# Self attentions: the four transfers of the row sums go from SyncE's queue to GpSimd's, one in each unit

## The reference

```python
x = x + attention_with_position_bias(layernorm(x))   # self attention A
x = x + cross_block(layernorm(x), ctx_1024, mask)    # cross attention, self attention S, feed-forward
x = x + experts(layernorm(x))                        # 8 experts, top 2
# in each self attention, for batch b and head h:
probs = softmax(q_h @ k_h.T * SCALING [+ bias_h])    # 256 x 256
out_h = probs @ v_h                                  # 256 x 8
```

## Time and profile before

| | |
|---|---|
| median of three runs | 1294.16 us (1292.65 to 1294.98) |
| the profiled execution's own time | 1292.28 us |
| its span, first to last instruction | 1290.3 us |
| busy: PE, DVE, ACT, POOL | 1077.4, 995.1, 860.7, 406.4 us |
| mean granted TensorE clock | 0.92 of full speed |

### The profile page before, as it was taken

How to read it: one execution, slowest core, us unless ns; L and a number is a source line. 1 busy time by engine, 2 the same in 40 slices (tenths; PEclk the granted TensorE clock), 3 DMA queues, 4 the chain that set the end, 5 groups by cost and what they waited for, 6 DMA issues and landing times. The chain is left out here.

```text
span 1290.3 us, 32652 instructions
## 1 busy us (share of the span) xinstructions
PE 1077.4 (83%) x11660; PEld 576.5 (45%) x11660; DVE 995.1 (77%) x2779; ACT 860.7 (67%) x1764; POOL 406.4 (31%) x832
## 2 busy tenths in 40 slices
PE   5779995699999999999999999997667878539993
PEld 2334443244444444444444444443433445428883
DVE  7458766588889888898888988992777968766664
ACT  3468883087888878877788787785357965425553
POOL 3211213214150230502305023011442515755662
PEclk8689998689999999999999999998878999759997
DMA  6934015523223132231322303100373012301113
GB/s 164 219 70 96 24 29 139 139 65 78 61 55 98 55 79 62 62 95 51 79 62 60 95 27 79 53 5 3 103 148 63 14 46 94 106 13 40 46 48 115
DMA packets 82974, 94.84 MB, mean 73 GB/s; under 512 B 12775, under 2 KB 69039, under 8 KB 82816
## 3 DMA queue, kind: packets, MB, share of 16 engines
q1 hardware_dynamic: 78720, 86.46, 26.7%
q0 software_dynamic: 2496, 5.12, 1.5%
q10 hardware_dynamic: 1600, 1.18, 0.4%
HBM read 66.47 MB, written 27.48 MB: 73 GB/s over the span
## 5 line engine op out<-in xcount | busy, mean ns | idle before, releaser
L1558 DVE TENSOR_REDUCE MG<-bank 128x1 f32<-128x401 f32 (+1 forms) x1024 | 515.4, 566 | 75.2 <-PE bank L1342 73.3
L1478 ACT ACTIVATE PT<-bank 128x512 f32<-128x512 f32 (+1 forms) x624 | 334.7, 597 | 64.2 <-PE bank L1360 63.6
L1360 PE MATMUL bank<-QP,KP 54*128 54x256 bf16 (+1 forms) x1664 | 252.5, 274 | 16.2 <-DVE CAT L1573 4.1
L1342 PE MATMUL bank<-KP,QP 54*128 54x401 bf16 (+1 forms) x1024 | 237.1, 344 | 14.7 <-DMA KP<-ctx_k_parts 9.5
L1380 PE MATMUL bank<-PT,VP 128*9 128x256 f32 (+1 forms) x2688 | 198.2, 368 | 0.8 <-ACT XT L1478 0.8
L1633 POOL TENSOR_TENSOR MP<-MN,ZERO 128x4 bf16<-128x4 f32 x128 | 26.4, 206 | 440.9 <-DVE MN L1565 435.9
L1360 PEld LDWEIGHTS bank<-QP,KP 54*128 54x128 bf16 (+1 forms) x1664 | 110.6, 96 | 108.1 <-ACT PT L1478 24.4
L1342 PEld LDWEIGHTS bank<-KP,QP 54*128 54x128 bf16 x1024 | 75.5, 94 | 125.0 <-DVE MG L1558 93.2
L1004 PE MATMUL bank<-QP,KP 51*128 51x256 bf16 x512 | 97.9, 285 | 39.1 <-DMA QP<-q_parts 12.5
L1478 ACT ACTIVATE XT<-bank 128x512 f32<-128x512 f32 (+1 forms) x208 | 116.2, 599 | 20.3 <-PE bank L1360 19.9
L971 PE MATMUL bank<-KP,QP 51*128 51x256 bf16 x512 | 100.7, 294 | 3.9 <-DVE MG L1099 1.0
(11 more groups left out here) (283 smaller groups left out, 1870.7 us busy)
## 6 DMA issues: line engine op xcount, KB each, us to landing
KP<-ctx_k_parts SPq DMA_DIRECT2D x128, 100.1 KB
ctx_k_parts<-KPARTS SPq DMA_DIRECT2D x16, 600.4 KB, 5.3
KP<-ctx_k_parts SPq DMA_DIRECT2D x128, 59.4 KB
CN<-in_ctx SPq DMA_DIRECT2D x8, 768.0 KB
RAW<-in_w_gate_up SPq DMA_DIRECT2D x8, 512.0 KB, 3.7
QP<-q_parts SPq DMA_DIRECT2D x20, 192.0 KB
ctx_k_parts<-KPARTS SPq DMA_DIRECT2D x16, 200.1 KB, 5.4
UQ<-bias_table SPq DMA_DIRECT2D x4, 768.0 KB, 8.3
```

The source lines that it names most:

```text
L1342: nc.tensor.matmul(GRAIN[n % NG][:, 0:w], k.QP[half, p, b * S + 128 * qt:b * S + 128 * (qt + 1)], k.KP[half, p, a:a + w], start=True, stop ...
L1360: return nc.tensor.matmul(bank[0:rows[t], S * at:S * (at + 1)], k.KP[half, p, 128 * t:128 * t + rows[t]], k.QP[half, p, b * S:(b + 1) * S] ...
L1478: nc.scalar.activation(PT[n % NP][0:rows[t], :], bank_of("s", g, t)[0:rows[t], :], ACT.Exp).then_inc(exp_done, 1)
L1558: nc.vector.tensor_reduce(MG[:, g % 4, 2 * s + qt, chunk:chunk + 1], GRAIN[n % NG][:, 0:w], AX.X, ALU.max).then_inc(m_read, 1)
```

## The change

The four functions issue on GpSimd (`nc.gpsimd.dma_start`, and the waits on GpSimd's stream) instead of SyncE. GpSimd's plan gets an entry behind the split: in step s, for s from 4 to 31, the stage s mod 4 (take, spread, give, place) of batch s // 4 - 1. So there is one transfer in a unit, behind that unit's split. SyncE's loads of the chunks 1 to 3 stand one behind another, in A the mask transfers follow as one run, and in S nothing comes after the loads.

```diff
-        take, spread, give, place = sums
-
-        def place_mask(b):
+        for c in range(1, 4):
+            sp.wait_ge(self.stored[c], 64)
+            load_keys(k, sp, 0, c, qk_in[c])
+            load_queries(k, sp, 0, c, qk_in[c])
+        sp.wait_ge(self.mask_stored, 32)
+        for b in range(B):
             for s in range(2):
                 src = bass.AP(tensor=flat.tensor, offset=b * NCTX, ap=[[B * NCTX, 3], [0, PAIRS], [1, NCTX]])
                 sp.dma_start(k.dC.ap()[b, s, 4 * HD:, :, :], src).then_inc(self.mask_placed, 16)
-
-        sp.wait_ge(self.stored[1], 64)
-        load_keys(k, sp, 0, 1, qk_in[1])
-        take(sp, 0)
-        load_queries(k, sp, 0, 1, qk_in[1])
-        spread(sp, 0)
-        sp.wait_ge(self.stored[2], 64)
-        load_keys(k, sp, 0, 2, qk_in[2])
-        give(sp, 0)
-        load_queries(k, sp, 0, 2, qk_in[2])
-        place(sp, 0)
-        take(sp, 1)
-        sp.wait_ge(self.stored[3], 64)
-        load_keys(k, sp, 0, 3, qk_in[3])
-        spread(sp, 1)
-        load_queries(k, sp, 0, 3, qk_in[3])
-        give(sp, 1)
-        sp.wait_ge(self.mask_stored, 32)
-        place_mask(0)
-        place(sp, 1)
-        for b in range(2, LAST_BATCH):
-            take(sp, b)
-            spread(sp, b)
-            place_mask(b - 1)
-            give(sp, b)
-            place(sp, b)
-        place_mask(LAST_BATCH - 1)
-        place_mask(LAST_BATCH)
         sp.wait_ge(self.mask_placed, 16 * 2 * B)
...
-            if c == 3:
-                take(sp, 0)
-                spread(sp, 0)
             sp.wait_ge(self.stored[c], 64)
             load_keys(k, sp, 2, c, qk_in[c])
-            if c == 3:
-                give(sp, 0)
             load_queries(k, sp, 2, c, qk_in[c])
-        place(sp, 0)
-        for b in range(1, LAST_BATCH):
-            take(sp, b)
-            spread(sp, b)
-            give(sp, b)
-            place(sp, b)
...
-    pool_plan = [("split", 0, 3)]
+    pool_plan = [("split", 0, 3), ("move", 0, 0)]
...
+                elif what == "move":
+                    if PER_BATCH <= step < UNITS and what in actions:
+                        actions[what](step // PER_BATCH - 1, step % PER_BATCH)
...
+        def take_sums(pl, b):
+
+            pl.wait_ge(o_read, PER_BATCH * (b + 1))
             if b > 0:
+                pl.wait_ge(sums_in, 16 * b)
             a = PER_BATCH * b % NO
+            nc.gpsimd.dma_start(k.dSums.ap().rearrange("(u c) n -> c u n", c=4),
                          OT[HD:128:32, a:a + PER_BATCH, :]).then_inc(sums_out, 16)
 
+        def spread_sums(pl, b):
+
+            pl.wait_ge(sums_out, 16 * (b + 1))
             if b > 0:
+                pl.wait_ge(compact_done, b)
+            nc.gpsimd.dma_start(SUMS[:, 0, :], compact(k.dSums)).then_inc(sums_in, 16)
+
+        def give_reciprocals(pl, b):
+
+            pl.wait_ge(compact_done, b + 1)
             if b > 0:
+                pl.wait_ge(rec_in, 16 * b)
+            nc.gpsimd.dma_start(compact(k.dRec), SUMS[:, 1, :]).then_inc(rec_out, 16)
+
+        def place_reciprocals(pl, b):
+
+            pl.wait_ge(rec_out, 16 * (b + 1))
             if b > 0:
+                pl.wait_ge(sums_done, b)
             src = bass.AP(tensor=k.dRec.ap().tensor, offset=0, ap=[[S, H], [0, HD], [1, S]])
+            nc.gpsimd.dma_start(REC, src).then_inc(rec_in, 16)
...
+            def move(b, stage):
+                (take_sums, spread_sums, give_reciprocals, place_reciprocals)[stage](pl, b)
+
+            run(pool_plan, {"split": split_maxima, "move": move})
```

More of the change, by code:

```diff
@@ L536, in store_item, with sync @@
                     self.stored[c])
-    def sync(self, sp, qk_in, sums):
+    def sync(self, sp, qk_in):
         k, I = self.k, self.k.ins
@@ L896, in ot @@
             return OT[:, u % NO, :]
-        def take_sums(sp, b):
-            sp.wait_ge(o_read, PER_BATCH * (b + 1))
+        def take_sums(pl, b):
+            pl.wait_ge(o_read, PER_BATCH * (b + 1))
             if b > 0:
-                sp.wait_ge(sums_in, 16 * b)
+                pl.wait_ge(sums_in, 16 * b)
             a = PER_BATCH * b % NO
-            sp.dma_start(k.dSums.ap().rearrange("(u c) n -> c u n", c=4),
+            nc.gpsimd.dma_start(k.dSums.ap().rearrange("(u c) n -> c u n", c=4),
                          OT[HD:128:32, a:a + PER_BATCH, :]).then_inc(sums_out, 16)
-        def spread_sums(sp, b):
-            sp.wait_ge(sums_out, 16 * (b + 1))
+        def spread_sums(pl, b):
+            pl.wait_ge(sums_out, 16 * (b + 1))
             if b > 0:
[L911 to L916, removed]
+                pl.wait_ge(compact_done, b)
+            nc.gpsimd.dma_start(SUMS[:, 0, :], compact(k.dSums)).then_inc(sums_in, 16)
+        def give_reciprocals(pl, b):
+            pl.wait_ge(compact_done, b + 1)
             if b > 0:
[L918 to L923, removed]
+                pl.wait_ge(rec_in, 16 * b)
+            nc.gpsimd.dma_start(compact(k.dRec), SUMS[:, 1, :]).then_inc(rec_out, 16)
+        def place_reciprocals(pl, b):
+            pl.wait_ge(rec_out, 16 * (b + 1))
             if b > 0:
-                sp.wait_ge(sums_done, b)
+                pl.wait_ge(sums_done, b)
             src = bass.AP(tensor=k.dRec.ap().tensor, offset=0, ap=[[S, H], [0, HD], [1, S]])
-            sp.dma_start(REC, src).then_inc(rec_in, 16)
+            nc.gpsimd.dma_start(REC, src).then_inc(rec_in, 16)
         def copy_maxima(copy, eng, u, heads, done):
@@ L1169, in split_maxima @@
                     front.prepare(u - UNITS // 2)
-            run(pool_plan, {"split": split_maxima})
+            def move(b, stage):
+                (take_sums, spread_sums, give_reciprocals, place_reciprocals)[stage](pl, b)
+            run(pool_plan, {"split": split_maxima, "move": move})
         @block.sync
         def _(sp):
-            front.sync(sp, qk_in, (take_sums, spread_sums, give_reciprocals, place_reciprocals))
+            front.sync(sp, qk_in)
 V_BURSTS = (range(0, 4), range(4, 8), range(8, NTILES))
```

## The result

The changed kernel takes 1312.2 us (median of 4 runs, 1308.15 to 1313.9) against 1294.57 us before (4 runs, 1292.65 to 1295.32): a ratio of 1.0136, 95% interval 1.0115 to 1.0157. The prediction had the sign and the range (1290 to 1315), but forecast about 8 us over the median where 17.6 came. The profiled execution took 1313.23 us, of which 1311.4 are its span, against 1292.28 and 1290.3; 21.1 us of span are to be found (of the changed kernel's four runs, the profiled one is the second slowest).

The account below looks back on a forecast made before the run. TensorE was taken to bound the first self attention, VectorE the second, with queue waits at batch 0. First -7.2 us, second +16.1, sum +8.9, gave 1302.2 us; range 1290 to 1315.

Parts of the forecast that it names:

- The waits removed: Batch 0 stretches: TensorE's wait for queries in the first attention (-9.86 us), VectorE's in the second (-7.41 us) go.
- The traffic beside batches 0 and 1 of the first attention: GpSimd's transfers there run beside SyncE's remaining loads and masks: +1.5 us for both batches, between 0 and 3.
- The end of the first attention: Batch 6's chain starts only behind the last split, delaying the last long reciprocal: +1.2 us (0 to 3.2).
- Batch 0 of the second attention: The 7.41 us go, 2.32 us of new waits come, with 1.0 for loads beside it: -4.1 us.
- Batches 1 to 5 and the end: Second attention: VectorE waits 2.32 us a batch, 11.6 for five; bias additions 4.9; last long reciprocal 3.7 later.
- the bias rows: Second attention, units 16 to 23: GpSimd's addition delays four awaited transfers by 1.22 us each, 4.9 us.
- x: Extra time of a transfer issued from GpSimd over one from SyncE: taken as 0.5 us, range 0 to 1.
- 8.56 + 4x: Each attention's end: the last batch's chain of transfers and reciprocal behind the last split, in us.
- What was to show it: Second attention: waits about 1 us each, over 2 in middle batches; batches of 14.9 us and more instead of 12.57.
- The clock's rival: Second attention: short waits drop TensorE's clock to the lower level, 17 us on top, 1319 us; chance 0.05.
- descriptors held up by VectorE: Rival: GpSimd's descriptors wait for VectorE or are written slowly, x = 1, 1315.6 us; chance 0.08.
- The fifth rival: First attention: chunk 1's queries are late for another reason, TensorE waits as before, 1311 us; chance 0.05.

Follow-up runs that it names:

- reordered: Kernel before with only SyncE's queue order changed: first attention's chunk 1 queries ahead of batch 0's transfers, later loads placed behind or between transfers: 1276.54 us, ratio 0.987.
- hold: Changed kernel with second attention's transfers back on SyncE and first attention's SyncE loads from chunk 2 on held until batch 0's reciprocals land: 1293.36 us, ratio 1.0011.
- spaced: Changed kernel with second attention's transfers back on SyncE and first attention's later loads and masks spread out behind its transfers: 1285.84 us, ratio 0.9955.
- s_paced2: Kernel before, but second attention's SyncE transfers each wait for the unit's split, chunk 3's loads one at a time behind them: 1300.08 us, ratio 1.0043.
- s_paced: Kernel before, but second attention's SyncE transfers each wait for the unit's split, with chunk 3's loads all ahead: 1309.42 us, ratio 1.0116.

## Why the prediction was half right

- **The waits removed** (-9.86 and -7.41 us): the sizes are right, as the reordered kernel shows. SyncE stood at the head of its queue, and with another order it doesn't.
- **The traffic beside batches 0 and 1 of the first attention: the step that failed.** The prediction took 1.5 us, "between 0 (covered as above) and 3 (two transfers in each late by 0.75)". It measured 9.46 us, all in batch 0. The transfer times that I used were those of transfers with nothing beside them. I had noted that the masks would "move ahead into one burst" and that batches 0 and 1 run beside it, but I sized this by no row, and asked who waits for the burst, not what it does to the take. The trace of before had rows to go by: DMA shares of 0.71 and 0.79 in 78 to 90 us, and, in the second attention, reciprocals that landed after 4.4 instead of 2.4 us beside a share of 0.72 (issued at 980.02 us). hold and spaced show that it was the burst. The Trainium skill (DMA: Bandwidth & Descriptors, section "Issuing engines are not separate DMA queues") says in the same place that transfers started by different engines interleave on the same 16 engines; I weighed only its other half, on issue time, against the trace. The half that I left out is what the 9.20 us of the take show; the other half leaves out a wait at the head of an engine's program: with the take on another engine the queries were issued 11.2 us earlier (65.45 for 76.66).
- **The end of the first attention**: forecast +1.2, measured +0.1 (from the end of the last split to the last long reciprocal 9.91 us, 9.81 before).
- **Batch 0 of the second attention**: forecast -4.1, or -2.9 for the table's start to r1, where batch 1's sums are waited for too (1.20); measured +0.7 (46.91 to 47.62). The same fault: 1.0 us was set for the loads beside it. SyncE issues chunk 3's loads from 970.12 to 978.73 us, the DMA share is 0.54 in 970 to 976, and the sums spread at 971.31 are seen 4.24 us later. With these loads spread out and the same place of the transfers, but on SyncE's queue, s_paced2 needs 41.06 us, 5.9 less than before; no run spread them out beside GpSimd's.
- **Batches 1 to 5 and the end**: 2.32 us a batch for four batches, 4.9 for the bias rows and 4.8 from r5 to the end (1.12 for batch 5's reciprocals, and 3.7) make 19.0; 11.95 + 5.33 = 17.3 came. The one batch without the addition in its waits (r4 to r5, 15.08) is 2.51 longer than before, against 2.32. The bias rows cost 0.47, 1.09 and 0.43 more in the three others, 2.0 in place of 4.9: an addition puts the issue off by 0.87 us (1.16 less 0.29), not 1.22, and the sums behind the addition were seen 1.93 and 2.63 us after their issue, the others 2.77 to 3.18, so part of the delay is made good. Why was not tried.
- **x can't be told from the scatter.** I used 2.48 us for SyncE's sums (1048.33 to 1050.81); that was an upper bound, since VectorE was at work until then. Where VectorE does wait for SyncE in the second attention, it sees them after 1.56 to 1.76 us in three rows (s_paced at 984.11 and 1067.31, s_paced2 at 1057.30) and after 3.42 to 3.78 us in three others (s_paced at 1027.52, s_paced2 at 1011.04 and 1043.13); in the first attention's last batch after 2.41 (before) and 2.62 (reordered). GpSimd's, behind batch 0, take 1.93 to 3.48. For the reciprocals x is nil: from both queues most land after 2.3 to 2.5 us. By the chains at the two ends, 9.39 and 10.90 us from the last split's end to the scaling against 8.56 + 4x, x is 0.2 and 0.6. That 2.32 a batch came near the truth is in part luck: its base was too long, and it had neither the gaps before the issue nor TensorE's part in it.
- **What was to show it.** Batches of 14.9 us and more came (15.08 to 16.17), and waits of 1.10 to 1.67 us at nearly each transfer, but none over 2 in the middle batches. The prediction called itself wrong if GpSimd's transfers landed within 2.4 us; the reciprocals did (2.3, once 3.2), and the waits came all the same, because 0.29 to 1.16 us between the split's end and the issue (998.10 to 998.39, 1013.65 to 1014.81) are to be added before the 1.78 us are used up. I had no term for the gap. TensorE did not come to wait for the splits (in batches 1 to 5 its weight loads wait 2.2 us for them in all, 3.4 before).
- **Rivals.** The clock's rival came true in a small part: I had held against it that it took 6 us of standing, but stands of 1.6 to 2.1 us were followed by the lower level four times, and VectorE waited 2.49 us for TensorE in these places (0.20, 0.72, 0.54 and 1.03). Of descriptors held up by VectorE the rows show nothing: the issues last 0.53 to 0.85 us, and the reciprocals land as early as SyncE's. The fifth rival, that the wait for the queries stays, was wrong as it stood, though its 1311 us came nearest: the first attention gained nothing, but by another wait.

Summed: first attention +0.4 for -7.2, second +18.0 for +16.1, and 2.7 us of span elsewhere that no step foresaw. The second attention's sum lies near in part by luck: it had 3.6 us too little for batch 0 and 1.7 too much behind it.

## What to carry to other kernels

A wait at the head of a queue can be cured by the order within that queue; first see whether the transfers behind can go past, before another queue is taken. A small transfer on a queue of its own is no longer ahead of the large ones: it shares the transfer engines with all that the other queue may now issue at once, so price it from a stretch with the same traffic, not from a quiet one. And a transfer's place in an in-order engine's program is worth as much as its latency: ask how long before its use it is issued, and take a latency only from rows where the reader did wait, and from several: 1.6 and 3.8 us stood side by side.

## What was not expected of the hardware

Apart from batch 0, the 128 KB of reciprocals land either after 2.3 to 2.5 us or after 2.9 to 3.8, on either queue. The view of transfers shows what differs. Here it is for two of the kernel before's, both issued by SyncE (at 1019.28 and 1052.62 us), the last line with the time to landing:

```profile
DMA packets 144, 0.13 MB, mean 44 GB/s; under 512 B 16, under 2 KB 144, under 8 KB 144
...
q1 hardware_dynamic: 144, 0.13, 13.1%
...
REC<-head_reciprocals SPq DMA_DIRECT2D x1, 128.0 KB, 2.4
```

```profile
DMA packets 145, 0.15 MB, mean 36 GB/s; under 512 B 16, under 2 KB 144, under 8 KB 144
...
q1 hardware_dynamic: 144, 0.13, 10.8%
q8 instruction: 1, 0.02, 2.0%
...
REC<-head_reciprocals SPq DMA_DIRECT2D x1, 128.0 KB, 3.6
```

In the second a packet of the instruction queue q8 (0.02 MB, on one of the 16 engines) falls into the transfer's time. In the profiles of before, after, s_paced, s_paced2 and reordered there are 35 transfers of this kind in the second attention. Of 22 without such a packet (from 0.5 us before the issue to 3.5 behind it) 21 landed within 2.5 us and one, beside a DMA share of 0.72, after 4.4; of 13 with one 10 took 2.9 to 3.8 and 3 took 2.4. The other five kernels say the same: of 21 without one 18 landed within 2.5 us and three, beside DMA shares of 0.82 to 0.90, after 4.8 to 6.1; of 14 with one 11 took 2.6 to 3.6 and 3 took 2.3 to 2.4. That the packets of q8 come over the same 16 engines and can hold back part of a small transfer by 0.5 to 1.4 us (2.9 to 3.8 against 2.4) fits most of these; it is a coincidence in time, and no run took the packet away. It may also be why s_paced and s_paced2, with the same place, differ by 1.2 us a batch: in s_paced2 three of the seven transfers of reciprocals met one, in s_paced one took 3.6. Between issue and sight the three late spreads of row sums on SyncE (3.42 to 3.78 us) have such a packet each, and the three early ones none.
